# Expert mask products over all 128 rows, the last group's gate behind the ninth to twelfth tile, residuals moved, GpSimd idle behind the gates

## The reference

```python
y1 = _ln(x + _mha(x, ...), ln1_g, ln1_b)
gates = softmax(y1 @ wg); idx = argmax(gates); mask1 = one_hot(idx, E)
loc = sum((cumsum(mask1, 0) - 1.0) * mask1, -1); keep = loc < cap      # cap = 512 tokens an expert
h = einsum('ecd,edf->ecf', disp, w1) + b1; y = einsum('ecf,efd->ecd', h, w2) + b2
moe = where(keep, gate_val * y[slot], 0.0)
y2 = _ln(y1 + moe, ln2_g, ln2_b)
out = x0 + _layernorm(y2)
```

## Time and profile before

| what | us |
|---|---|
| device time, median of 3 runs | 661.74 (660.5 to 662.3) |
| device time of the profiled execution | 663.98 |
| its span, first to last instruction | 662.3 |
| PE busy in the span (x3475) | 546.7 (83%) |
| DVE busy (x882) | 535.4 (81%) |
| ACT busy (x773) | 393.8 (59%) |
| POOL busy (x326) | 219.5 (33%) |

### The profile page before, as it was taken

One profiled execution on the slowest core, in us unless ns is written; L12 is line 12 of the kernel. 1 busy time (PEld: TensorE's weight loads), 2 busy tenths in 40 slices (PEclk: granted clock), 3 DMA queues, 4 the chain that ended last, 5 costly groups with the idle time before them and its releaser, 6 DMA issues.

```text
span 662.3 us, 9804 instructions
## 1 busy us (share of the span) xinstructions
PE 546.7 (83%) x3475; PEld 195.2 (29%) x3475; DVE 535.4 (81%) x882; ACT 393.8 (59%) x773; POOL 219.5 (33%) x326
## 2 busy tenths in 40 slices
PE   2784899999999999999999987766779999898600
PEld 1560122222222222222222224645565334122100
DVE  4869799999999999999999923799775843289986
ACT  1651598998898888988889863535533001025333
POOL 7001020178034450354403660835653000014441
PEclk9996599999999999999999999979879989696555
DMA  9842010111111121211221001100000000000102
GB/s 242 256 137 112 13 40 21 41 35 52 48 60 31 34 55 46 67 27 31 59 55 53 7 10 42 38 0 2 1 1 1 0 1 0 0 0 1 32 21 75
DMA packets 31393, 28.94 MB, mean 44 GB/s; under 512 B 6240, under 2 KB 23784, under 8 KB 31344
## 3 DMA queue, kind: packets, MB, share of 16 engines
q1 hardware_dynamic: 29312, 27.33, 14.4%
q10 hardware_dynamic: 2032, 0.98, 0.6%
HBM read 19.23 MB, written 8.65 MB: 42 GB/s over the span
## 4 chain that ended last, share of the span: by engine, by line
PE 49%; DVE 31%; POOL 7%; ACT 6%; issue 4%; DMA 2%; ACTq 0%; SPq 0%; DVEq 0%
PE ps L1490 13%; PE ps L1485 10%; DVE row_max L1662 9%; PE ps L607 7%; PE ps L1458 5%; DVE space L948 3%; DVE space L889 2%; PE ps L605 2%; ACT attended L1610 2%; PE ps L614 2%; DVE space L275 1%; ACT space L1594 1%; PE ps L562 1%; DMA w_in<-in_L_ffn_out_proj_w 1%; DVE space L1056 1%
## 5 line engine op out<-in xcount | busy, mean ns | idle before, releaser
L1662 DVE TENSOR_REDUCE row_max<-ps 128x2 f32<-128x1024 f32 x256 | 299.5, 1219 | 16.3 <-PE ps L1458 13.5
L1594 ACT ACTIVATE space<-ps 128x512 f32<-128x512 f32 x512 | 271.7, 605 | 47.8 <-PE ps L1485 47.4
L1485 PE MATMUL ps<-space 51*128 51x512 bf16 x512 | 158.8, 387 | 6.6 <-ACT space L1594 3.3
L1490 PE MATMUL ps<-space 128*32 128x512 f32 x1024 | 138.1, 612 | 3.0 <-ACT space L1594 0.7
L1458 PE MATMUL ps<-space 48*128 48x512 bf16 x512 | 128.0, 399 | 14.2 <-DVE row_max L1662 12.5
L1485 PEld LDWEIGHTS ps<-space 51*128 51x128 bf16 x512 | 41.0, 94 | 164.6 <-ACT space L1594 144.9
L607 PE MATMUL ps<-W,space 128*128 128x512 f32 x128 | 87.3, 770 | 0.0
L1334 POOL CAST max_parts<-row_max 128x16 bf16<-128x16 f32 x32 | 6.3, 197 | 238.3 <-DVE row_max L1662 238.3
L948 DVE TENSOR_REDUCE space<-ps 128x128 f32<-128x1024 f32 x32 | 38.9, 1221 | 42.3 <-PE ps L607 42.3
L444 POOL TENSOR_TENSOR space<-PC,same_row 128x512 f32<-128x512 f32 x32 | 33.0, 1061 | 36.2 <-DVE PC L903 28.3
L454 POOL TENSOR_TENSOR space<-space,rows 128x512 f32<-128x512 f32 x24 | 30.0, 1270 | 41.1 <-DVE space L275 22.9
(11 more groups left out here) (220 smaller groups left out, 641.2 us busy)
## 6 DMA issues: line engine op xcount, KB each, us to landing
q_parts_dram<-space SPq DMA_DIRECT2D x2, 1536.0 KB, 5.4
space<-q_parts_dram SPq DMA_DIRECT2D x64, 48.0 KB
attended_dram<-attended SPq DMA_DIRECT2D x128, 18.0 KB
X<-in_L_attn_queries SPq DMA_DIRECT2D x8, 256.0 KB, 7.6
space<-in_L_ffn_w SPq DMA_DIRECT2D x2, 1024.0 KB, 5.9
space<-q_parts_dram SPq DMA_DIRECT2D x64, 32.0 KB
space<-attended_dram SPq DMA_DIRECT2D x16, 128.0 KB, 2.4
space<-inverses_dram SPq DMA_DIRECT2D x16, 128.0 KB
```

Of the source, the lines that this page charges most:

```text
L1485: pe.matmul(ps[:, col_bank(v), :], k_rows[rows_a, kappa // 4 % 2, tc * P:(tc + 1) * P], q_stack[rows_a, kappa % 4, b * S:(b + 1) * S], sta ...
L1490: mm = pe.matmul(ps[32 * m:32 * m + 32, PV, :], v_heads[:, tc, PAIR * (kappa // 4) + m % PAIR, :], probs[:, tc % 2, m, :], start=(tc == 0) ...
L1594: act.activation(probs[:, tc % 2, m, :], ps[:, col_bank(v), :], ACT.Exp, scale=1.0 / math.sqrt(DH)).then_inc(s_pr, 1)
L1662: dve.tensor_reduce(row_max[:, par].rearrange("p (a c) -> p a c", a=PAIR)[:, :, item], ring(n), AX.X, MAX).then_inc(s_free, 1)
```

## The change

Mask products: `others` moves to the (by then unused) space of w1T and has a slot of its own for each tile pair, zero outside that pair's 32 rows, so that the mask product runs over all 128 rows; DVE writes a group with four copies of 32 rows. Norms: the root takes 1/D and epsilon in its own scale and bias, two of the seven small operations go (L262, L266), and all norms are applied as x * inv + shift, for which the small operation behind the reciprocal, so far only in the norms of the end (L1068), now stands in all of them. Residuals 0 and 1 stand earlier on DVE. On PE route(2), the turning of y1 and route(3) stand between tiles 8 and 11, the counts are taken behind tile 11, and DVE does the gate ahead of select(12) in place of behind select(21). POOL has no work behind `affine1(2)`: `sum_up`, `affine2` and `last_residual` of groups 0 to 2 are on DVE, between its selects. The order of the roots and applications on ACT follows.

```diff
+        others = w1T[:].rearrange("p a c d -> p (a c d)").bitcast(BF16).rearrange("p (g k t) -> p g k t", g=G, t=P)
...
             ch.done(dve.scalar_tensor_tensor(small[:, 4, :], diff, D / 4.0, diff, MUL, MUL))
-            ch.done(dve.tensor_scalar(mean, mean, 0.5, None, MUL))
-            ch.wait()
-            ch.done(dve.tensor_tensor(var, var, small[:, 4, :], ADD))
-            ch.wait()
-            dve.tensor_scalar(var, var, 1.0 / D, EPS, MUL, ADD).then_inc(s_var, 1)
-
-        def norm_invert(dve, ch, k, small):
+            ch.wait()
+            dve.tensor_tensor(var, var, small[:, 4, :], ADD).then_inc(s_var, 1)
+
+        def norm_invert(dve, ch, k, small, ready=None):
             dve.wait_ge(s_sd, k + 1)
             ch.done(dve.reciprocal(small[:, 3, :], small[:, 2, :]))
             ch.wait()
+            ins = dve.scalar_tensor_tensor(small[:, 4, :], small[:, 0, :], -0.5, small[:, 3, :], MUL, MUL)
+            if ready is None:
+                ch.done(ins)
+                ch.wait()
+            else:
+                ins.then_inc(ready, 1)
 
         def norm_apply(dve, src, dst, small, which=range(B)):
             for b in which:
-                ins = dve.tensor_scalar(dst(b), src(b), small[:, 0, b:b + 1], small[:, 3, b:b + 1], SUB, MUL)
+                ins = dve.tensor_scalar(dst(b), src(b), small[:, 3, b:b + 1], small[:, 4, b:b + 1], MUL, ADD)
...
-        TAIL = [(4, 0), (4, 1), (5, 0), (4, 2), (5, 1), (4, 3), (5, 2), (5, 3)]
+        TAIL = [(4, 0), (4, 1), (5, 0), (5, 1), (4, 2), (5, 2), (4, 3), (5, 3)]
...
-            act.activation(small[:, 2, :], small[:, 2, :], ACT.Sqrt).then_inc(s_sd, 1)
+            act.activation(small[:, 2, :], small[:, 2, :], ACT.Sqrt, scale=1.0 / D, bias=eps[:]).then_inc(s_sd, 1)
...
-            sum_up(1)
-            affine2(0)
-            sum_up(2)
-            affine2(1)
-            last_residual(0)
-            affine2(2)
-            last_residual(1)
-            last_residual(2)
...
-                bank, rows_k, variant = expert_bank(k), slice(32 * (b // 2), 32 * (b // 2) + 32), b % 2
+                bank = expert_bank(k)
                 for half in range(2):
                     cols = slice(half * 512, half * 512 + 512)
-                    pe.matmul(ps[:, bank + half, :], others[rows_k, g, :], c_stack[rows_k, variant, cols],
+                    pe.matmul(ps[:, bank + half, :], others[:, g, b // 2, :], c_stack[:, b % 2, cols],
...
             turn_y1(2)
-            tile(8)
-            tile(9)
-            route(2)
-            tile(10)
-            tile(11)
-            turn_mask(2)
-            for k in range(12, 16):
-                tile(k)
-            for half in range(2):
-                if half == 0:
-                    pe.wait_ge(s_lgc, 3)
-                else:
-                    pe.wait_ge(s_nm, 3)
+            def turn_last(half):
                 pe.wait_ge(s_y1l, half + 1)
                 for b in range(QB):
-                    mm = pe.transpose(ps[:, 6 + half, b * P:(b + 1) * P], A[:, G - 1, QB * half + b, :], ident[:])
+                    mm = pe.transpose(ps[:, 7 - half, b * P:(b + 1) * P], A[:, G - 1, QB * half + b, :], ident[:])
                 mm.then_inc(s_y1t, 1)
-                tile(16 + half)
+
+            tile(8)
+            route(2)
+            turn_last(0)
+            tile(9)
+            pe.wait_ge(s_lgc, 3)
+            turn_last(1)
+            tile(10)
             route(G - 1)
-            tile(18)
-            tile(19)
+            turn_mask(2)
+            tile(11)
             turn_mask(G - 1)
-            pe.wait_ge(s_lgc, G)
+            pe.wait_ge(s_nm, QB * 3)
             masks = maskp[:].rearrange("p g k c -> p (g k) c")[:, :, MASK_ROW:MASK_ROW + 2 * E]
             pe.matmul(ps[:, 6, 0:T * E], upper[:], masks, start=True, stop=True)
             pe.matmul(ps[:, 6, T * E:2 * T * E], all_ones[:], masks, start=True, stop=True).then_inc(s_cnt, 1)
-            for k in range(20, T):
+            for k in range(12, T):
...
-            weigh(1)
             root4(0)
             apply4(0)
-            weigh(2)
+            weigh(1)
             root4(1)
-            apply4(1)
             root5(0)
             apply5(0)
+            apply4(1)
+            weigh(2)
+            root5(1)
             root4(2)
+            apply5(1)
             apply4(2)
-            root5(1)
-            apply5(1)
+            root5(2)
+            apply5(2)
             root4(3)
             apply4(3, range(0, B, 2))
-            root5(2)
-            apply5(2)
             root5(3)
...
-                dve.tensor_scalar(others[:, g, :], turned_mask(g), -1.0, 1.0, MUL, ADD).then_inc(s_nm, 1)
+                if g == 0:
+                    dve.wait_ge(s_oz, 1)
+                for k in range(QB):
+                    rows_k = slice(32 * k, 32 * k + 32)
+                    ins = dve.tensor_scalar(others[rows_k, g, k, :], turned_mask(g)[rows_k, :], -1.0, 1.0, MUL, ADD)
+                    ins.then_inc(s_nm, 1)
...
+            residual(0)
             dve.wait_ge(s_r1, G)
             norm_variance(dve, ch, tiles(A, last), st6o, smallo)
-            residual(0)
             variance1(0)
             norm_invert(dve, ch, LAST1, smallo)
             ch.done(norm_apply(dve, tiles(A, last), tiles(A, last), smallo))
@@ -971,8 +949,8 @@
             norm_apply(dve, tiles(X, last), tiles(A, last), smallo).then_inc(s_n2l, 1)
             normalise(4)
             compact(5)
+            residual(1)
             normalise(5)
-            residual(1)
...
-            for k in range(8, 11):
-                select(k)
+            select(8)
             choose(2)
+            select(9)
+            select(10)
+            choose(g)
+            copy_others(2)
             select(11)
-            copy_others(2)
-            for k in range(12, 20):
-                select(k)
-            choose(g)
-            select(20)
             copy_others(g)
-            select(21)
...
+            def affine2(g):
+                dve.wait_ge(s_n4, g + 1)
+                ch.done(dve.tensor_tensor(A[:, g], A[:, g], bcast(rows[:, 2, :], B), MUL))
+                ch.wait()
+                ch.done(dve.tensor_tensor(A[:, g], A[:, g], bcast(rows[:, 3, :], B), ADD))
+                ch.wait()
...
+            def sum_up(g):
+                dve.wait_ge(s_wa, g)
+                ch.done(dve.tensor_tensor(same(A[:, g]), same(A[:, g]), same(YT[:, g]), ADD))
+                ch.wait()
+
+            def last_residual(g):
+                dve.wait_ge(s_n5, g + 1)
+                dve.tensor_tensor(same(A[:, g]), same(A[:, g]), same(X[:, g]), ADD).then_inc(s_y2, 1)
...
+            select(12)
             for b in range(B):
                 ins = weigh(b)
             ch.done(ins)
             ch.wait()
+            select(13)
             variance4(0)
+            select(14)
+            scale4(0)
+            select(15)
+            select(16)
+            select(17)
+            affine2(0)
+            select(18)
+            sum_up(1)
+            select(19)
+            variance4(1)
+            select(20)
+            variance5(0)
+            select(21)
+            scale4(1)
+            scale5(0)
+            select(22)
+            select(23)
+            last_residual(0)
             last_tile(0)
+            affine2(1)
             last_tile(1)
+            variance5(1)
             last_tile(2)
+            sum_up(2)
             last_tile(3)
+            scale5(1)
+            variance4(2)
             last_tile(4)
+            scale4(2)
             last_tile(5)
+            last_residual(1)
             last_tile(6)
+            affine2(2)
             last_tile(7)
+            variance5(2)
+            scale5(2)
 
...
             norm_smalls(dve, ch, st64(g), small4(g))
-            scale4(g)
+            norm_invert(dve, ch, tail(4, g), small4(g), s_i4)
+            dve.wait_ge(s_i4, G)
             ch.done(norm_apply(dve, tiles(A, g), tiles(A, g), small4(g), odd))
-            variance5(2)
-            ch.wait()
-            dve.wait_ge(s_n4, G)
-            ch.done(dve.tensor_tensor(A[:, g], A[:, g], bcast(rows[:, 2, :], B), MUL))
-            ch.wait()
-            dve.tensor_tensor(A[:, g], A[:, g], bcast(rows[:, 3, :], B), ADD).then_inc(s_aff, 1)
-            scale5(2)
+            last_residual(2)
+            ch.wait()
+            affine2(g)
             variance5(g)
             scale5(g)
+            dve.wait_ge(s_i5, G)
             ch.done(norm_apply(dve, tiles(A, g), tiles(A, g), small5(g), odd))
...
+                if kappa == 5:
+                    pool.wait_ge(s_wu, E)
+                    pool.memset(others, 0.0).then_inc(s_oz, 1)
```

More of the change, by code:

```diff
@@ L161, in build @@
         neg_half = sb("neg_half", [P, B])
+        eps = sb("eps", [P, 1])
         v_tmp = sb("v_tmp", [P, TC, D])
@@ L217, in build @@
              "logits_ready", "logits_copied", "expert_masks_ready", "gate_exp_done", "tokens_counted", "weights_ready"))
```

(43 more changed lines are left out.)

28 lines of the change are left out of this document (7 added, 21 removed).

## The result

| what | before | after |
|---|---|---|
| device time, median, runs side by side | 661.12 us | 622.66 us (620.53 to 624.94, 4 runs) |
| ratio, 95% interval | | 0.9426 (0.9375 to 0.9477) |
| span of the profiled execution | 662.3 us | 621.3 us (device time 623.81) |
| mean granted clock | 0.906 | 0.948 |

The change saves 38.5 us. The forecast of 631 us (624 to 648) is 8.3 us too high, and the range ends 1.3 us above the result.

A forecast was written before the change was run, and what follows sets the result against it. PE was taken to bound the expert tiles ahead of the gate, DVE everything behind it. The last addition moves from 658.6 to 627.6 us, -31.0, giving 633.0 for the profiled execution and a median of 631 us, range 624 to 648.

The forecast's parts named there:

- Same columns, so I take 0 for PE: Mask products on 128 rows: no change in PE's time, bounds 0 to 1 us of cost.
- Expert tile 8, with which the first stage of the earlier trace begins.: Mark for PE's tiles ahead of the gate: tile 8 starts at 525.9 us, not 529.9.
- Two stretches at 1.2 GHz: PE between tile 8 and the gate: two slow-clock stretches of 3.4 us, costing 1.6 us each, 3.1 in all.
- Behind the gate: DVE from gate to last addition: 74.1 us of summed work plus 3 us of waits for PE, 77 against 71.8.
- the waits for ACT at the end stay what they are: DVE's waits for ACT behind the gate: unchanged, nothing added to the sum.
- The front: Stages ahead of tile 8, with residuals moved earlier: 4 us saved, bounds 2 and 6.
- The early gate: Gate ahead of select(12): done at 550.5 instead of 586.8 us, 36.3 earlier, with ten more selects behind it, +11.8.
- 11.8 + 13.5 - 20.9 - 2.1: DVE behind the gate: ten more selects, work from POOL, less stalls, weighing and single stalls, less dropped small operations.
- rival C: DVE behind the gate: stalls are not POOL's alone, half of the 20.9 us stays, 641 us; chance 0.05.
- Rivals B: PE behind the gate: clock falls again and again, last tile at 623, total 646 us; chance 0.17.
- E: PE stays at 1.2 GHz from tile 8 on, last tile at 652.6, total 675 us, slower; chance 0.04.
- Rival D: Gate not early, as choose(3) or the counts wait for something queued: 10 us later, 641 us; chance 0.04.

The follow-up runs named there:

- masks on 128 rows: Kernel before with the mask products on 128 rows, the four copies of a group and the memset, nothing else: 648.59 us against 663.87, ratio 0.9771.
- gate late: Kernel after with PE's order behind tile 7 and choose(3), the gate and what follows back at their old places: 639.48 us.
- the runs with memsets and with additions: Kernel after plus, on POOL from the gate on, 18 memsets of 128x1024 (622.80 us) or 18 additions of 128x512 on its own data (629.43 us).

## Why the prediction was right or wrong

**Where the gain came from.** The runs give one path from before to after, stage by stage: masks on 128 rows -16.1 us (2.6 + 13.5); residuals, with the norms' fewer small operations ahead of tile 0, -3.2 (the average of 113.5 against before's 116.75); the end with POOL idle, fewer small operations and ScalarE's new order -5.5 (71.86 to 66.32, before against gate late); the early gate -17.1; the rest, 0.8 the other way, is that the attention ended later in the trace of after (380.17 against 379.39). Together -41.1, and 40.9 were seen. On another path the shares differ: put in last, the masks are worth 4.8. Only the 3.2 hangs on an average over traces that spread by 4 us.

**Where the forecast missed.** It had -31.0 for the span. The 9.9 us too little are, in its own steps:

- *"Same columns, so I take 0 for PE", bounds "0 to 1 us": the step that failed.* The runs show a gain, 4.8 us in this order and 16.1 in the old one. The working saw the 0.1 us in the open beside the mask product and took it as something more rows could only add to. It ruled out a gain without a reason. The two starts of 0.31 and 0.53 in the earlier trace rows held three open loads a half, and all three went. The price was looked for only "while PE is the bound", which is right, but that held for tiles 0 to 7 as well: -2.7 there, -2.0 from tile 8 to the gate.
- *"Expert tile 8, with which the first stage of the earlier trace rows begins."* That is tile 9. The eight transposes at 525.29 end at 526.33, and tile 8 starts there. So the stage up to the gate was 3.6 us longer before than the forecast thought, and all of it was to be gained: -3.6.
- *"Two stretches at 1.2 GHz", 3.1 us:* none came. The rest of the stage from tile 8 to the gate was 1.3 us longer than summed, of which the copies are 0.4: four of them took 0.96 us and not 0.6. With four tiles of 2.15 in place of 2.75 (-2.4) the stage is 20.4 us against 24.6: -4.2, the -2.0 above within it.
- *Behind the gate* 77.1 was forecast and 75.9 measured: -1.2. The wait for PE was taken as 3 us, and DVE waited 0.2 for it in 20 selects. Against that, the forecast had "the waits for ACT at the end stay what they are", and they grew from 3.9 us to 5.7. So the small miss of this stage is two larger ones that cancel in part, which is luck.
- *The front* was forecast at -4: measured -3.2, and the attention ended 0.8 later: +1.6.

-2.7 - 3.6 - 4.2 - 1.2 + 1.6 = -10.1, which is the miss to 0.2 us. Nearly half of it, 4.7, is the first step; the rest is a misread mark, a clock that didn't fall, and sizes.

**What held.** project(3) was to start at 463.4 and started at 464.21 with everything 0.8 us later; its eight matmuls took 3.70 us where 4.25 were taken. The early gate was the right lever, with its price of ten selects behind it. DVE's busy time from the gate on was to grow by 2.3 us (11.8 + 13.5 - 20.9 - 2.1) and grew by 2.1 (39.07 + 26.87 = 65.9 in the earlier trace rows, 45.78 + 3.30 + 19.00 = 68.1 after). So the stalls went as summed: rival C (half of the 20.9 us stays) is out by that and by small operations of 0.17 us, and the runs with memsets and with additions say that they were POOL's. Rivals B and E had PE's last tile at 623 and 652, and its last product with W started at 592.5. Rival D is out by the gate at 541.8.

**Pages and rows.** The forecast set the Trainium skill, Perfetto Trace Analysis (Optimizing Scalar/DVE Operations), against its sum: that work taken off a saturated DVE may help, even on GpSimd. Here moving it back costs 3.6 us, by waits for POOL's results and by held operations. The Trainium skill, TensorE: Matmul & The Clock Gate (Part 4), says that transposes don't count as busy for the clock; by that the tiles between them should run slower. Eight of them and two routes stood between tiles 8 and 11 and the granted clock stayed 1.00, so no loss of that kind is seen here. The eight take 1.2 us in all, too little to say more than that.

## What to carry to other kernels

A product on fewer than all 128 rows, put between products on all rows, is not cheap because it is small: if there is zero space to pad its operand to 128 rows, try that wherever PE is the bound, and count the gain only over the stretch where it is. Before pricing a change, give "the same work in another shape" a bound on both sides, and hold the time of a mark (here tile 8's start) against the end of what stands ahead of it. Work handed from VectorE to GpSimd can cost VectorE twice, in the wait for its result and in the operations that its reads hold; and once an engine paces the end, look at what stands ahead of the last group's short operations on the other engines.

## What the runs showed of the hardware that was not expected

- A bf16 product of 32 or of 64 rows costs 0.3 us more than one of 128 rows when it stands between fp32 products of 128 rows at 2.4 GHz: 1.37 against 1.08 us for the three. Its own record is no longer (0.39 us against 0.38); the time is in the gaps to its neighbours, also between the two fp32 matmuls behind it. The Trainium skill, TensorE: Matmul & The Clock Gate (Why this matters for your kernels), says that a single product over 32 rows takes the same time as one over 128. The product's own record agrees; a sequence like this one takes longer, and for it the measurement decides.
- VectorE's operation with two SBUF inputs goes at the pace of GpSimd's reads, about one for each GpSimd operation: eight weighings in 8.08 us beside additions of 1.18 us each (21.20 / 18). In that run reductions from PSUM and the statistics beside them are untouched, and memsets held nothing.
- The granted clock stayed at 1.00 from 491 to 590 us across routes and transposes in the new order; nine of the ten traces of that order have no loss between tile 8 and the gate, and the one on 64 rows has 3.4 us. In the old order it fell behind both routes on 32 rows, and on 128 rows (masks on 128 rows, gate late) behind neither, but once at PE's wait of 2.5 us for choose(3), at 558.8 and 557.1. That the missing wait is what keeps it up in the new order was not tried apart.
